# Graph attention layer on one core: q and k of the first stage made for all heads at once and placed by DMA, LayerNorm 1 applied on GpSimd

## The chip, the core and the metric

The kernel runs on one core of one Trainium2 chip. The metric is device time in microseconds of one whole execution. The engines are TensorE (PE; its weight loads are shown as PEld), VectorE (DVE), ScalarE (ACT), GpSimd (POOL) and SyncE (SP). Each runs its own list of instructions in order, and they wait for one another by semaphores. DMAs are issued here by SP and by ACT.

## The reference, cut to what matters

The input is x (4096 x 128, float32) and a 4096 x 4096 integer adjacency matrix. There are 8 heads of 16.

```
qkv = layer_norm(x, g1, be1) @ w_qkv            # q, k, v: 4096 x 8 x 16
scores = einsum('nhd,mhd->hnm', q, k) * HEAD_DIM ** -0.5
attn = softmax(where(adj != 0, scores, -inf))   # over m
x = x + einsum('hnm,mhd->nhd', attn, v).reshape(n, DIM) @ w_proj + b_proj
out = x + gelu(layer_norm(x, g2, be2) @ w1 + b1) @ w2 + b2
```

## The kernel before

**Two parts.** A first stage makes what all later work needs: k of all 4096 rows (`k_stack`), v (`v_ones`), q of the first tile (`q_stack[0]`), the normalized rows transposed (`xnT_dram`) and the masks and row maxima of the first tile. After it, `run_iterations` goes over 8 tiles of 512 query rows. This part is not touched.

**How q and k lie.** Products are taken in float16 with each number split in a high and a low part. A pair of heads lies in 128 partitions, 64 for each head: rows 0 to 15, 16 to 31 and 35 to 50 of a half hold copies of the head's 16 numbers, high or low as `Q_LOW` and `K_LOW` say (`PART_ROW` gives the first rows), and rows 32 to 34 serve a shift by the row maximum. In `k_stack` two of those rows hold the constant `SHIFT_UNIT`. Each chunk of 512 keys in `k_stack` has 64 more columns ahead (`K_FIRST`), a second copy of some keys.

**The first stage before.** The rows are taken in 8 chunks of 512. Per chunk: DVE takes mean and variance (`stats1`), ACT the root (`root`, L695), DVE applies them (`apply1`, four instructions of 128x128, L368), PE transposes (`transpose_rows`, L1055), ACT copies with scale and bias (`transposed_rows`, L701) and stores the chunk to `xnT_dram`. Then PE multiplies it by a weight matrix in which a pair's columns are repeated in the layout above (`wk_rep`, L1105), once for each of the 4 pairs: an "item". ACT reads each item twice (L722 the negated high part, L724 the float32 number), and POOL adds the two into `k_stack` (L543, and L541 for the 64 more columns). The first q takes 4 items more, so there are 36. PE also makes v (`chunk_values`), which ACT copies (L727).

**What else runs there.** POOL turns 12 blocks of 128x1024 adjacency numbers into masks (`convert`, two instructions, L517 and L521), one after every second item; DVE makes the first four (`first_masks`, L873). SP loads the blocks into two buffers (L407) and transposes masks by DMA (L412). For the row maxima of the first tile PE makes scores of 128 rows by 512 keys (`first_row`, L1080), and DVE takes the masked maximum of each (`row_maximum`, L858): 8 such units per chunk, 7 steps behind the items (`ROW_LAG`). At the end come `negated_maxima` (L868), 20 units of row maxima more, and the first tile.

**The order** of each engine is that of the loops as written: there is no scheduler. An instruction that waits holds all behind it on its engine, and a DMA is issued in its place in the list of the engine that issues it.

## Time and profile before

| | |
|---|---|
| median of 3 runs | 1702.24 us (1699.94 to 1702.98) |
| the profiled execution | 1704.14 us, of which the span is 1702.3 us |
| busy in the span: PE, DVE, ACT, POOL | 93%, 83%, 75%, 69% |
| DMA moved | 125.88 MB |

The span goes from the first instruction to the last. The page divides it into 40 slices, so that the first stage, which ends near 105 us, is two and a half of them. Shares over the whole span say little on it; the rows below are therefore of windows. The page puts an idle time down to the engine that released it.

### The profile page before, as it was taken

To read this page: it belongs to the slowest core of one execution; us is meant where nothing else is said; L and a number is where in the kernel's file an instruction comes from. 1 tells how busy PE (TensorE), PEld (TensorE's weight loads), DVE (VectorE), ACT (ScalarE), POOL (GpSimd) and SP (SyncE) were. 2 spreads that over 40 slices of the span, in tenths; PEclk is the share of its full clock that TensorE was granted. 3 is DMA by queue.
4 is the path that set the end of the run, shared out by engine and by line. 5 is a ranking of instruction groups with operands and counts; after the bars stand their busy time and mean duration, and the time that the engine had idled before them with its cause. 6 is when DMAs were issued, how large, how long until landed. Compare 5 with 4: busy or idle time off the path is not lost.

```text
span 1702.3 us, 46524 instructions
## 1 busy us (share of the span) xinstructions
PE 1588.7 (93%) x17016; PEld 496.5 (29%) x17016; DVE 1419.3 (83%) x4490; ACT 1274.2 (75%) x1394; POOL 1167.4 (69%) x1092
## 2 busy tenths in 40 slices
PE   6989999999999999999999999999999999999996
PEld 3422222323223232232323232232323232232323
DVE  6888989987999889997898879998899879988811
ACT  4647878777777878778776877778787787868793
POOL 4955487569865798568875698567885688657551
PEclk9979999999999999999999999999999999999997
DMA  8810046301460046500462025700464015600000
GB/s 214 184 52 2 5 142 128 76 5 57 141 124 30 5 116 138 97 5 26 137 127 63 5 81 136 134 2 5 133 130 88 4 39 148 123 18 5 14 5 13
DMA packets 177856, 125.88 MB, mean 74 GB/s; under 512 B 140974, under 2 KB 155183, under 8 KB 177628
## 3 DMA queue, kind: packets, MB, share of 16 engines
q1 hardware_dynamic: 163196, 108.49, 26.7%
q10 hardware_dynamic: 14432, 14.42, 3.3%
q8 instruction: 135, 2.21, 0.5%
q14 instruction: 93, 0.76, 0.1%
HBM read 77.25 MB, written 6.04 MB: 49 GB/s over the span
## 4 chain that ended last, share of the span: by engine, by line
PE 52%; ACT 22%; issue 14%; POOL 8%; DVE 2%; ACTq 1%; DMA 1%; SPq 0%; POOLq 0%; DVEq 0%
ACT probs L820 20%; PE pv_ps L1149 15%; PE ring_ps L1080 10%; PE score_ps L1241 9%; PE score_ps L1256 9%; POOL probs L582 2%; PE ring_ps L1207 2%; PE score_ps L1173 2%; POOL k_stack L543 2%; ACT q_stack L689 1%; DVE masked_out L858 1%; PE ring_ps L1198 1%; PE ring_ps L1183 1%; PE ring_ps L1190 1%; POOL row_mask L517 1%
## 5 line engine op out<-in xcount | busy, mean ns | idle before, releaser
L858 DVE CUSTOM_DVE_ANT_0 masked_out<-ring_ps,row_mask 128x512 bf16<-128x512 f32 x2048 | 1311.9, 688 | 138.6 <-PE ring_ps L1080 99.3
L820 ACT ACTIVATE probs<-score_ps,score_scale 128x1024 f32<-128x1024 f32 x1010 | 1075.6, 1112 | 338.5 <-PE score_ps L1256 324.4
L582 POOL TENSOR_TENSOR probs<-probs,keep 128x1024 int32<-128x1024 int32 x256 | 604.2, 2361 | 252.1 <-ACT probs L820 241.6
L1149 PE MATMUL pv_ps<-probs,v_ones 128*17 128x512 f32 x4096 | 543.7, 599 | 4.6 <-POOL probs L582 4.0
L1080 PE MATMUL ring_ps<-k_stack,q_stack 51*64 51x512 f16 x4096 | 488.0, 397 | 15.1 <-DVE row_max L858 13.8
L1256 PE MATMUL score_ps<-q_stack,k_stack 51*64 51x512 f16 x4040 | 370.4, 391 | 18.9
L1080 PEld LDWEIGHTS ring_ps<-k_stack,q_stack 51*64 51x64 f16 x4096 | 169.0, 104 | 495.7 <-DVE row_max L858 446.2
L1241 PE MATMUL score_ps<-mask_t,ident_bf 64*64 64x512 bf16 x3028 | 274.9, 387 | 34.1 <-ACT probs L820 15.5
L1256 PEld LDWEIGHTS score_ps<-q_stack,k_stack 51*64 51x64 f16 x4040 | 115.6, 104 | 211.6 <-PE score_ps L1241 183.6
L858 DVE DVE_READ_ACCUMULATOR2_ANT row_max<- 128x1 f32 x2048 | 169.9, 83 | 0.0
L521 POOL TENSOR_SCALAR row_mask<-row_mask 128x1024 bf16<-128x1024 bf16 x124 | 129.5, 1045 | 23.6 <-POOL row_mask L517 23.0
L1241 PEld LDWEIGHTS score_ps<-mask_t,ident_bf 64*64 64x64 bf16 x3028 | 91.9, 105 | 182.8 <-ACT probs L820 134.1
L517 POOL TENSOR_SCALAR row_mask<-adj_in 128x1024 bf16<-128x1024 uint32 x124 | 129.0, 1040 | 4.2 <-DVE row_max L858 2.1
L1149 PEld LDWEIGHTS pv_ps<-probs,v_ones 128*17 128x17 f32 x4096 | 72.4, 95 | 141.7 <-issue 73.6
L526 POOL TENSOR_SCALAR max_unit<-neg_max 128x4 f32<-128x4 f32 x64 | 12.7, 198 | 78.8 <-DVE neg_max L868 78.1
L958 DVE RECIPROCAL recip<-ring_ps 128x16 f32<-128x16 f32 x16 | 4.1, 257 | 61.0 <-PE ring_ps L1183 61.0
L689 ACT COPY q_stack<-score_ps 2x256 f16<-2x256 f16 x128 | 46.5, 363 | 9.2 <-PE score_ps L1047 6.9
L975 DVE TENSOR_TENSOR rows<-ring_ps,x_res 128x128 f32<-128x128 f32 x32 | 9.3, 291 | 41.1 <-PE ring_ps L1207 41.1
L574 POOL TENSOR_SCALAR keep<-mask_t 128x512 int32<-128x512 bf16 x64 | 39.6, 619 | 5.4
L1173 PE MATMUL score_ps<-h2T,w_sb 128*128 128x512 f32 x64 | 38.0, 688 | 2.4 <-ACT h2T L755 1.0
L591 POOL TENSOR_SCALAR q_x<-q_x 128x512 f32<-128x512 f32 x14 | 8.7, 620 | 45.2 <-ACT q_x L765 45.1
L722 ACT ACTIVATE hidden<-score_ps,part_coef 128x512 f16<-128x512 f32 x36 | 28.0, 777 | 14.5 <-PE score_ps L1105 11.8
(128 smaller groups left out, 840.3 us busy)
## 6 DMA issues: line engine op xcount, KB each, us to landing
adj_in<-adj SPq DMA_DIRECT2D x128, 512.0 KB, 4.2
halves<-attn ACTq DMA_DIRECT2D x30, 128.0 KB, 2.7
q_stack<-q_dram SPq DMA_DIRECT2D x42, 64.0 KB
mask_t<-row_mask SPq DMA_TRANSPOSE x128, 3.5
xq<-xnT_dram ACTq DMA_DIRECT2D x8, 256.0 KB, 2.7
halves<-halves ACTq DMA_DIRECT2D x16, 128.0 KB, 2.2
x_res<-x ACTq DMA_DIRECT2D x8, 256.0 KB, 4.5
out<-rows ACTq DMA_DIRECT2D x8, 256.0 KB, 5.4
```

The source lines that it names most:

```text
L517: nc.gpsimd.tensor_scalar(target, adj_in[:, half, :].bitcast(U32), 1.0, 0.0, ALU.min, ALU.max)\
L521: nc.gpsimd.tensor_scalar(target, target, BIG, -BIG, ALU.mult, ALU.add).then_inc(mask_done, 1)
L574: nc.gpsimd.tensor_scalar(keep[:, KEPT.index(m), :], mask_t[:, m, :], 1.0 / BIG, 1.0, ALU.mult, ALU.add)\
L582: nc.gpsimd.tensor_tensor(view, view, keep[:, KEPT.index(m), :].unsqueeze(1).broadcast_to([128, 2, TILE]), ALU.mult).then_inc(probs_masked, 1)
L689: last = nc.scalar.copy(stack[r:r + SHIFT_PARTS, p, 256 * jj:256 * (jj + 1)], bank.bitcast(F16)[r:r + SHIFT_PARTS, 0:256])
L820: nc.scalar.activation(probs[:, (2 * g + n) % SLOTS, :], score_banks(i, place).rearrange("p a n -> p (a n)"), ACT.Exp, scale=score_scale[: ...
L858: nc.vector.tensor_tensor_reduce(out=masked_out[:, place % 3, :], in0=ring_ps[:, place % 3, :], in1=row_mask[:, j, ch * 512:(ch + 1) * 512 ...
L1080: last = nc.tensor.matmul(ring_ps[64 * t:64 * (t + 1), place % 3, :], stack[rows, p, first:first + 64], k_stack[rows, p, ch, K_FIRST:], st ...
L1149: last = nc.tensor.matmul(pv_ps[32 * k:32 * k + HD + 1, :], v_ones[:, block_of(g, b), 2 * p + a, :], probs[:, (2 * g + b) % SLOTS, a * TIL ...
L1173: last = nc.tensor.matmul(bank, w1_sb[:, 128 * f:128 * (f + 1)], h2T[:, :], start=True, stop=True)
L1241: last = nc.tensor.matmul(bank[to, :], ident_bf[keys, keys], mask_t[keys, source, :], start=True, stop=False)
L1256: last = nc.tensor.matmul(bank[64 * t:64 * (t + 1), :], k_stack[rows, p, m // 4, at + 64 * t:at + 64 * (t + 1)], q_stack[par][rows, p, :], ...
```

## The change

Items are now 9: one for q of the first chunk and one for k of each chunk, each a product with the plain weight matrix (`wq_all`, `wk_all`), all heads at once, 128 rows of 16 x 8 numbers. ACT copies the product twice (high part in float16, and the float32 number), POOL subtracts to get the low part, ACT stores both parts to `item_dram`, and loads them from there into the rows of `q_stack[0]` (6 DMAs) or `k_stack` (9 DMAs for a chunk, 3 of them for the 64 more columns). The constant rows of `k_stack` are set once by DVE and copied over by two DMAs; `q_stack[0]` is cleared by DVE. The four instructions that apply LayerNorm 1 move from DVE to POOL. The masks that POOL makes come in pairs after an item. The row maxima run 8 steps behind instead of 7, and there are 4 steps to a chunk as before. The six instructions that filled the repeated weights, and POOL's clearing of them, are gone. The diff, cut:

```
+FIRST_PER = 4
+ITEMS = 1 + CHUNKS
 DEPTH = 4
-ROW_LAG = 7
+ROW_LAG = 8
-POOL_FIRST_MASKS = {4 + 2 * k: 4 + k for k in range(CONVERTED - 4)}
+POOL_FIRST_MASKS = {n: (2 * n + 2, 2 * n + 3) for n in range(1, 7)}
...
+            def apply1(c):
+
+                pool.wait_ge(rstd_done, c + 1)
+                if c >= 2:
+                    pool.wait_ge(stage_full, 2 * (c - 2) + 1)
+                settled(pool)
+                for s in range(SUB):
+                    nc.gpsimd.tensor_scalar(xn_rows[c % 2][:, s, :], x_all[:, c * SUB + s, :], mean_var[:, s, 0:1],
+                                            rstd[:, s:s + 1], ALU.subtract, ALU.mult).then_inc(ln1_applied, 1)
+
+            apply1(0)
             for n in range(ITEMS):
...
                 pool.wait_ge(item_read, n + 1)
...
-                nc.gpsimd.tensor_tensor(dst, item_x[n % DEPTH], item_neg[n % DEPTH], ALU.add).then_inc(item_done, 1)
...
+                nc.gpsimd.tensor_tensor(item_part[n % DEPTH][1], item_x[n % DEPTH], item_part[n % DEPTH][0],
+                                        ALU.subtract).then_inc(item_done, 1)
+                if n < CHUNKS - 1:
+                    apply1(n + 1)
+                for k in POOL_FIRST_MASKS.get(n, ()):
...
+            def take_item(n):
+
+                act.wait_ge(item_full, n + 1)
+                if n >= DEPTH:
+                    act.wait_ge(item_stored[n - DEPTH], 32)
+                nc.scalar.copy(item_part[n % DEPTH][0], score_ps[:, n % 4, :])
+                nc.scalar.copy(item_x[n % DEPTH], score_ps[:, n % 4, :]).then_inc(item_read, 1)
+
+            def store_item(n):
+                act.wait_ge(item_done, n + 1)
+                for low in range(2):
+                    act.dma_start(item_dram[n, low], item_part[n % DEPTH][low]).then_inc(item_stored[n], 16)
+
+            def load_item(n):
+
+                act.wait_ge(item_stored[n], 32)
+                for m, first in enumerate(PART_ROW):
+                    low = Q_LOW[m] if n == 0 else K_LOW[m]
+                    heads = item_dram[n, low].rearrange("(p a d) n -> a d p n", a=2, d=HD)
+                    for a in range(2):
+                        rows = slice(HALF * a + first, HALF * a + first + HD)
+                        to = q_stack[0][rows, :, :] if n == 0 else k_stack[rows, :, n - 1, K_FIRST:]
+                        act.dma_start(to, heads[a]).then_inc(item_in[n], 16)
+                    if n > 0:
+                        act.dma_start(k_stack[rows, :, n - 1, 0:K_FIRST],
+                                      heads[1][:, :, 128 * 2 + 64:128 * 3]).then_inc(item_in[n], 16)
...
+            for c in range(CHUNKS):
+                transposed_rows(c)
+                if c == 1:
+                    load_item(0)
+                if c >= 1:
+                    load_item(c)
+                if c + 1 < CHUNKS:
                     root(c + 1)
...
+                if c == 0:
+                    take_item(0)
+                take_item(c + 1)
+                act.wait_ge(stage_full, 2 * c + 2)
+                nc.scalar.copy(v_ones[:, c * SUB:(c + 1) * SUB, :, 0:HD],
+                               pv_ps[:, :].rearrange("p (s h d) -> p s h d", s=SUB, h=HEADS)).then_inc(v_done, 1)
+                if c == 0:
+                    store_item(0)
+                store_item(c + 1)
+            load_item(CHUNKS)
...
             for a in range(2):
-                nc.vector.memset(q_stack[1][HALF * a + SHIFT_ROW:HALF * (a + 1), :, :], 0.0).then_inc(q_clear, 1)
+                nc.vector.memset(k_stack[HALF * a + SHIFT_ROW:HALF * (a + 1), 0, 0, :], SHIFT_UNIT).then_inc(unit_set, 1)
+                for stack in q_stack:
+                    nc.vector.memset(stack[HALF * a + SHIFT_ROW:HALF * (a + 1), :, :], 0.0).then_inc(q_clear, 1)
...
                 if st >= ROW_LAG:
                     ch, j = divmod(st - ROW_LAG, SUB)
-                    pe.wait_ge(item_done, PAIRS * (ch + 1) + 1)
+                    if st == ROW_LAG:
+                        pe.wait_ge(unit_in, 32)
+                        pe.wait_ge(item_in[0], 16 * (Q_LOADS - 2))
+                    if j == 0:
+                        pe.wait_ge(item_in[ch + 1], 16 * (3 * len(PART_ROW)))
```

ACT's list before, from one transposed chunk to the next (chunk 2 to chunk 3; `hidden` and `probs` are the item's two copies, `attn` and `halves` the transposed chunks):

```order
L701 ACTIVATE halves<-pv_ps,gb 128x512 [waits stage_full]
L704 DMA xnT_dram<-halves 128x512 [waits xnT_ready]
L722 ACTIVATE hidden<-score_ps,part_coef 128x512 [waits item_done,item_full]
L724 COPY probs<-score_ps 128x512
L695 ACTIVATE rstd<-inv_var 128x4 [waits ln1_step]
L722 ACTIVATE hidden<-score_ps,part_coef 128x512 [waits item_done,item_full]
```

The same place in the list of the changed kernel, up to the stores of the next item:

```order
L705 ACTIVATE halves<-pv_ps,gb 128x512 [waits stage_full]
L708 DMA xnT_dram<-halves 128x512 [waits xnT_ready]
L732 DMA k_stack<-item_dram 16x4x512 [waits item_stored2]
L732 DMA k_stack<-item_dram 16x4x512
L734 DMA k_stack<-item_dram 16x4x64
L732 DMA k_stack<-item_dram 16x4x512 x2
L734 DMA k_stack<-item_dram 16x4x64
L732 DMA k_stack<-item_dram 16x4x512 x2
L734 DMA k_stack<-item_dram 16x4x64
L699 ACTIVATE rstd<-inv_var 128x4 [waits ln1_step]
L715 CAST hidden<-score_ps 128x512 [waits item_full]
L716 COPY probs<-score_ps 128x512
```

The root of the next chunk (L699) now stands behind a wait for the item's stores and nine DMA issues. After it come L761 (v) and the two stores L721, of which the first waits for POOL's `item_done`.

POOL's list before, over one mask (`hidden`, `probs` as above):

```order
L541 TENSOR_TENSOR k_stack<-probs,hidden 128x64 [waits item_read]
L543 TENSOR_TENSOR k_stack<-probs,hidden 128x512
L517 TENSOR_SCALAR row_mask<-adj_in 128x1024 [waits adj_loaded1]
L521 TENSOR_SCALAR row_mask<-row_mask 128x1024 [waits flag_done]
L541 TENSOR_TENSOR k_stack<-probs,hidden 128x64 [waits item_read]
L543 TENSOR_TENSOR k_stack<-probs,hidden 128x512
```

And POOL's list in the changed kernel, from the subtraction of item 2 to that of item 3 (`x_res` holds the normalized rows of chunk 3):

```order
L545 TENSOR_TENSOR hidden<-probs,hidden 128x512 [waits item_read]
L538 TENSOR_SCALAR x_res<-probs,mean_var,rstd 128x128 [waits rstd_done,stage_full]
L538 TENSOR_SCALAR x_res<-probs,mean_var,rstd 128x128 x3
L513 TENSOR_SCALAR row_mask<-adj_in 128x1024 [waits adj_loaded0]
L517 TENSOR_SCALAR row_mask<-row_mask 128x1024 [waits flag_done]
L513 TENSOR_SCALAR row_mask<-adj_in 128x1024 [waits adj_loaded1]
L517 TENSOR_SCALAR row_mask<-row_mask 128x1024 [waits flag_done]
L545 TENSOR_TENSOR hidden<-probs,hidden 128x512 [waits item_read]
```

Between two subtractions stand the four applications, which wait for ACT's root, and a pair of masks.

## Rows read from the trace of the kernel before

**Rows 1.** Busy time by window, us: PE, PEld, DVE, ACT, POOL, clock, DMA share, GB/s.
```profile
30.00:86.00 56.00, 51.20 (x270) 23.93 (x270) 49.67 (x154) 35.28 (x62) 52.24 (x65) 0.91 0.79 183
```

**Rows 2.** Groups of POOL up to 110 us: shapes, count | busy us, mean ns | idle before.
```profile
L543 POOL TENSOR_TENSOR k_stack<-probs,hidden 128x512 f16<-128x512 f32 x32 | 37.1, 1158 | 0.0
L521 POOL TENSOR_SCALAR row_mask<-row_mask 128x1024 bf16<-128x1024 bf16 x12 | 12.6, 1047 | 2.3 <-POOL row_mask L517 2.3
L517 POOL TENSOR_SCALAR row_mask<-adj_in 128x1024 bf16<-128x1024 uint32 x12 | 12.5, 1043 | 0.0
L541 POOL TENSOR_TENSOR k_stack<-probs,hidden 128x64 f16<-128x64 f32 x32 | 9.8, 306 | 6.6 <-ACT probs L724 5.6
```

**Rows 3.** Timeline of the first stage, start us, us: one mask on POOL, next item.
```profile
30.85 1.04 POOL L517 TENSOR_SCALAR row_mask<-adj_in 128x1024 bf16<-128x1024 uint32 x1
32.08 1.05 POOL L521 TENSOR_SCALAR row_mask<-row_mask 128x1024 bf16<-128x1024 bf16 x1 [0.19 <-POOL row_mask L517]
33.21 0.31 POOL L541 TENSOR_TENSOR k_stack<-probs,hidden 128x64 f16<-128x64 f32 x1
```

**Rows 4.** Timeline of the start and the end of the first stage.
```profile
19.24 0.20 ACT L695 ACTIVATE rstd<-inv_var 128x4 f32<-128x4 f32 x1 [1.89 <-DVE inv_var L364]
16.79 0.69 DVE L873 TENSOR_SCALAR row_mask<-adj_in 128x1024 bf16<-128x1024 int32 x1 [4.34 <-DMA adj_in<-adj]
101.72 1.15 POOL L543 TENSOR_TENSOR k_stack<-probs,hidden 128x512 f16<-128x512 f32 x1
103.78 0.69 DVE L858 CUSTOM_DVE_ANT_0 masked_out<-ring_ps,row_mask 128x512 bf16<-128x512 f32 x1
104.39 0.08 DVE L858 DVE_READ_ACCUMULATOR2_ANT row_max<- 128x1 f32 x1
```

**Rows 5.** DVE's application of LayerNorm 1: alone, and beside POOL (timeline).
```profile
10.47 1.11 DVE L368 TENSOR_SCALAR rows<-probs,mean_var,rstd 128x128 f32<-128x128 f32 x4
71.51 3.52 DVE L368 TENSOR_SCALAR rows<-probs,mean_var,rstd 128x128 f32<-128x128 f32 x4
```

**Rows 6.** One line's instructions: count, ns min/median/max; POOL's application of LayerNorm 2.
```profile
L631 POOL TENSOR_SCALAR rows<-x_res,mean_var,rstd x28: 787/791/798, 357.8 to 1539.4; 128x128 f32<-128x128 f32 x28
```

**Rows 7.** DMA issues, the same view, each with its issues' time to landing.
```profile
L704 ACTq DMA_DIRECT2D xnT_dram<-attn x4: 326/329/359, 14.0 to 67.5; - x4
DMA to landing us min/median/max: 2.0/3.1/5.5
...
L787 ACTq DMA_DIRECT2D halves<-attn x15: 614/620/1547, 225.5 to 1599.2; - x15
DMA to landing us min/median/max: 2.5/2.9/6.2
```

**Rows 8.** Timeline of SP: six loads of q from DRAM in the layout of the stacks.
```profile
233.02 3.50 SPq L484 DMA_DIRECT2D q_stack<-q_dram  x6
1410.79 2.69 SPq L484 DMA_DIRECT2D q_stack<-q_dram  x6
```

**Rows 9.** Groups of ACT and DVE up to 110 us.
```profile
L724 ACT COPY probs<-score_ps 128x512 f32<-128x512 f32 x36 | 20.8, 578 | 0.0
L701 ACT ACTIVATE attn<-pv_ps,gb 128x512 f32<-128x512 f32 x4 | 3.1, 784 | 10.8 <-PE pv_ps L1055 10.8
L914 DVE MEMSET q_stack<- 32x1024 uint32 x2 | 1.8, 912 | 1.3 <-PEq L1308 1.0 <-issue 0.3
```

**Rows 10.** Timeline of the first work of POOL and DVE.
```profile
3.36 0.87 DVE L356 BATCH_NORM_STATS2 stats<-probs 128x6 f32<-128x128 f32 x4 [0.27 <-DMA probs<-x]
17.43 1.15 POOL L543 TENSOR_TENSOR q_stack<-probs,hidden 128x512 f16<-128x512 f32 x1 [14.83 <-ACT probs L724]
```

More of the change, by code:

```diff
@@ L312, in program @@
         wqkv = probs[:, 5, 0:3 * DIM]
-        wq_rep = probs[:, 5, 3 * DIM:3 * DIM + PAIRS * 128].rearrange("p (q r) -> p q r", r=128)
         xn_rows = [rows2[:, :, :], x_res[:, :, :]]
         xnT = [attn[:, 0, :], attn[:, 1, :], halves[:, 0, :], halves[:, 1, :]]
-        item_neg = [hidden[:, n // 2, 256 * (n % 2):256 * (n % 2) + 256].bitcast(F16) for n in range(DEPTH)]
+        item_part = [[hidden[:, 2 * low + n // 2, 256 * (n % 2):256 * (n % 2) + 256].bitcast(F16) for low in range(2)]
+                     for n in range(DEPTH)]
         item_x = [probs[:, 6 + n // 2, TILE * (n % 2):TILE * (n % 2) + TILE] for n in range(DEPTH)]
@@ L364, in layer_norm_stats @@
             nc.vector.reciprocal(inv_var[:, :], inv_var[:, :]).then_inc(chain, 1)
-        def layer_norm_apply(chain, src, dst):
-            for s in range(SUB):
-                nc.vector.tensor_scalar(dst[:, s, :], src[:, s, :], mean_var[:, s, 0:1], rstd[:, s:s + 1],
-                                        ALU.subtract, ALU.mult).then_inc(chain, 1)
         def settled(eng):
@@ L706, in _ @@
+            act.wait_ge(unit_set, 2)
+            for a in range(2):
+                own = k_stack[HALF * a + SHIFT_ROW:HALF * a + SHIFT_ROW + SHIFT_PARTS + 1, :, :, :]\
+                    .rearrange("r p c k -> r (p c) k")
+                act.dma_start(own[:, 1:, :], own[:, 0:1, :].broadcast_to([SHIFT_PARTS + 1, PAIRS * CHUNKS - 1, K_CHUNK]))\
+                  .then_inc(unit_in, 16)
             root(0)
-            act.wait_ge(q_clear, 2)
+            act.wait_ge(q_clear, 4)
             act.wait_ge(w_in, 16 * 5)
-            act.wait_ge(consts_in, 16 * 4)
+            act.wait_ge(consts_in, 16 * 3)
@@ L924, in _ @@
             for st in range(FIRST_STEPS):
-                blk, k = st // PAIRS, st % PAIRS
+                blk, k = divmod(st, FIRST_PER)
                 if k == 0 and blk + 1 < CHUNKS:
@@ L929, in _ @@
                     first_masks(DVE_MASKS[st])
-                if k == 2 and blk + 1 < CHUNKS:
-                    apply1(blk + 1)
                 if st >= ROW_LAG:
@@ L1087, in first_row @@
                 row_scores(q_stack[0], u, j, p, a, ch)
-            pe.wait_ge(q_clear, 2)
+            pe.wait_ge(q_clear, 4)
             pe.wait_ge(scale_step, 4)
@@ L1092, in _ @@
             nc.tensor.matmul(score_ps[:, 0, 0:2 * DIM], ones_mat, w_sq, start=True, stop=True).then_inc(bound_full, 1)
-            pe.wait_ge(consts_in, 16 * 4)
-            pe.wait_ge(w_rep, 2 * len(PART_ROW) + 3)
+            pe.wait_ge(consts_in, 16 * 3)
+            pe.wait_ge(w_rep, 4)
             transpose_rows(0)
             for st in range(FIRST_STEPS):
-                blk, p = st // PAIRS, st % PAIRS
+                blk, p = divmod(st, FIRST_PER)
                 if p == 0 and 1 <= blk < CHUNKS:
                     transpose_rows(blk)
-                if st < ITEMS:
-                    chunk = max(blk - 1, 0)
-                    pe.wait_ge(xnT_ready, chunk + 1)
-                    if st >= 4:
-                        pe.wait_ge(item_read, st - 3)
-                    nc.tensor.matmul(score_ps[:, st % 4, :], (wq_rep if blk == 0 else wk_rep)[:, p, :],
-                                     xnT[chunk % 4], start=True, stop=True).then_inc(item_full, 1)
+                if p == 1 and blk < CHUNKS:
+                    pe.wait_ge(xnT_ready, blk + 1)
+                    for n in ((0, 1) if blk == 0 else (blk + 1,)):
+                        if n >= 4:
+                            pe.wait_ge(item_read, n - 3)
+                        nc.tensor.matmul(score_ps[:, n % 4, :], wq_all[:, :] if n == 0 else wk_all, xnT[blk % 4],
+                                         start=True, stop=True).then_inc(item_full, 1)
                 if st >= ROW_LAG:
                     ch, j = divmod(st - ROW_LAG, SUB)
-                    pe.wait_ge(item_done, PAIRS * (ch + 1) + 1)
+                    if st == ROW_LAG:
[3 more added lines that the diff above has]
+                        pe.wait_ge(item_in[ch + 1], 16 * (3 * len(PART_ROW)))
                     for x in range(2):
@@ L1114, in _ @@
                     chunk_values(blk).then_inc(stage_full, 1)
-            pe.wait_ge(item_done, ITEMS)
+            pe.wait_ge(item_read, ITEMS)
             for g in range(-LEAD, 0):
@@ L1289, in constants @@
 def constants():
-    c = np.zeros((128, 136), np.float32)
+    c = np.zeros((128, 132), np.float32)
     c[:, 0:128] = np.eye(128)
@@ L1293, in constants @@
         c[32 * k + HD, 128 + k] = 1.0
-    for r in range(128):
-        for n, first in enumerate(PART_ROW):
-            if first <= r % HALF < first + HD:
-                c[r, 132] = -Q_LOW[n]
-                c[r, 133] = -K_LOW[n]
-        if SHIFT_ROW <= r % HALF < SHIFT_ROW + SHIFT_PARTS:
-            c[r, 135] = SHIFT_UNIT
     return c
```

66 lines of the change are left out of this document (15 added, 51 removed).

## The prediction, made before the changed kernel was run

> **What bounds the kernel now.** The change touches only the first stage, so I read that stage and leave the tiles alone. First the windows: from 30 to 86 us, where the stage runs evenly, POOL is busy 52.24 of 56 us and DVE 49.67, ACT only 35.28 [rows 1]. Then the groups: POOL has 32 k items of 1.158 + 0.306 us and 12 masks [rows 2]. A mask takes 2.36 us from its start to the next instruction, 33.21 - 30.85 [rows 3]. A chunk costs POOL 4 x 1.46 + 1.5 x 2.36 = 9.4 us and the stage runs POOL nearly without a gap: its last item begins at 101.72, and the last of the row maxima that the stage gates ends at 104.39 + 0.08 = 104.47 us [rows 4]. So POOL bounds the stage now, with DVE close behind, and the change takes work from both. The question is what the time from 19.24 us, when the root of chunk 1 is taken [rows 4], to 104.47 us becomes.
>
> **What is removed.** POOL's items fall from 36 to 9, DVE loses 4 instructions a chunk that take 1.11 us alone and up to 3.52 us beside POOL [rows 5], ACT loses most of its item copies. By busy time alone the stage would be much shorter.
>
> **What is added, and where it stands.** ACT now issues for every chunk 2 stores and 9 loads, and it must wait for the stores to land before it loads. POOL has the four applications. Both are in order, and the order closes a circle through both engines. For chunk c: ACT takes the root of c; POOL, which waits for it, applies; POOL makes its pair of masks; only then POOL subtracts item c; ACT, which holds at the end of its step for this subtraction, stores the two parts; ACT copies the transposed chunk, waits for the landing, issues nine loads; and only behind these stands the root of c+1. Nothing in this circle lies beside another part of it, save ACT's copy beside the DMA's flight.
>
> **The circle in numbers.**
> - Application: 4 x 0.791 = 3.2 us, from POOL's same instruction on the same shape in LayerNorm 2, which varies only from 787 to 798 ns [rows 6].
> - Masks: 2 x 2.36 = 4.7 us [rows 3]. Their adjacency blocks were asked for a circle earlier, so no wait.
> - Subtraction: 1.16 us, that of L543 [rows 2], say 1.2.
> - Stores and landing: 0.1 for the semaphore, 0.5 for the first issue, and 3.0 from the second issue to landing: 3.6 us. ACT's own work meanwhile is two issues, the copy of 0.784 [rows 9] and its store of 0.33, about 2.3 us, and is covered. The landing is bounded from both sides by ACT's own queue: 2.0 to 5.5 us for 256 KB stores, 2.5 to 6.2 for 128 KB moves, medians 3.1 and 2.9 [rows 7]. I take 3.0. With 2.0 ACT's own 2.3 us would decide, 1.3 less; with 5.5, 2.5 more.
> - Nine loads: not in the trace on ACT. The nearest in form are SP's six loads of q, 2.69 to 3.50 us for six, so 0.45 to 0.58 each [rows 8]; ACT's own issues lie at 0.33 for whole tiles and 0.62 for the second of two half tiles [rows 7]. I take 0.48, nearest to the q loads: 4.3 us. Bounds 9 x 0.37 = 3.3 (0.33 and a gap) and 9 x 0.64 = 5.8.
> - Root and hand-over: 0.3 us.
> Sum 3.2 + 4.7 + 1.2 + 3.6 + 4.3 + 0.3 = 17.3 us a chunk. Before, the whole stage gave (104.47 - 19.24) / 8 = 10.7.
>
> On the landing, the Trainium skill (DMA: Bandwidth & Descriptors, "Anatomy of one DMA") puts one DMA at about 2.0 us fixed plus its bytes at 436 GB/s, on GpSimd's path. For 128 KB this gives 2.3 us, by which the circle would be 0.7 shorter and the sum below some 5 us less; the trace's medians of 2.9 and 3.1 [rows 7] are above it, with other queues busy.
>
> **The beginning.** The root of chunk 1 still comes at 19.24, as DVE waits for the second adjacency block till 16.79 before it [rows 4]. What is new ahead of it is hidden: two more clearings of 0.912 [rows 9] and two smaller ones push the first statistics from 3.36 [rows 10] to about 6, the application is in POOL's empty time (it is idle 14.83 us ahead of 17.43 [rows 10]), and chunk 0 has some 4 us to spare. If that cover is gone, for example because POOL needs longer for its first work, it costs up to 9 us. Then: two items copied, the first by 20.5 (2 x 0.578 [rows 9]); subtraction to 21.7; application to 24.9; second subtraction to 26.1; stores and transposed copy to 28.3; 6 + 9 loads of 0.48, 7.2 us, to 35.5; root 35.8; application 39.0; masks 43.7; item 2 is subtracted at 44.9.
>
> **The run and the end.** Items 3 to 7 follow at 17.3: 44.9 + 5 x 17.3 = 131.4. Then, with no masks and no application left: stores and landing 3.6, loads of chunk 6's keys 4.3, two copies 1.1, subtraction 1.2, stores and landing 3.6, nine loads 4.3, landing of the last 2.5 past its issue: 20.6, at 152.0. Then PE 0.4 and eight row maxima at the pitch of 0.61 (104.39 - 103.78 [rows 4]), 4.9: 157.3 us, where before stands 104.47. All behind it (negated maxima, 20 units, tiles) has the same instructions in the same order, and nothing there had waited for the first stage's other products: the last loads and mask transposes land while the row maxima run. So the change costs 52.8 us. Of the profiled execution's own 1704.14 us (span 1702.3 and 1.8 around it) that makes 1757; on the median of 1702.24, 1.9 lower, 1755. I give 1755.
>
> DVE's wait grows to half of each circle: it has 8 x 0.61 = 4.9 us of maxima and under 2 of statistics a chunk. PE is idle more, so its granted clock may be at its lower level here, as it partly is already (0.91 mean [rows 1]). Neither lies in the circle: PE's transposes run beside POOL's masks, its v beside ACT's loads.
>
> On moving the application, POOL's 3.2 us stands against 1.11 alone and 3.52 beside POOL on DVE [rows 5]: the step itself becomes no shorter, and it is now in the circle. The Trainium skill (Perfetto Trace Analysis, "Optimizing Scalar/DVE Operations") warns that GpSimd and VectorE share an SBUF port, so that moving work between the two might not help. The trace agrees, the same four instructions being three times as long beside POOL; it changes no term, since POOL's durations are what the sum uses.
>
> **Rivals.**
> - *The hand-over is cheap.* Issues of 0.37, landing inside ACT's own 2.3 us: the circle is 1.0 + 1.3 = 2.3 shorter, 7 landings and 7 ninefold loads behind item 2 make 16, the 15 loads ahead 1.7. The cost falls to 35: 1737. For it: the 0.33 of the whole-tile issues. Against: all strided issues on the two queues are 0.45 or more.
> - *The queue is crowded.* Issues of 0.64 and landings of 5.5: 1.5 + 2.5 more in seven places and 2.4 ahead, 30 more: 1785. For it: one L787 took 1.547 to issue and one landing 6.2 [rows 7], and the DMA engines are busy 0.79 of the time [rows 1]. Against: adjacency blocks and mask transposes are the bulk of that, and come once per circle, which makes them sparser; they are issued during POOL's masks, when ACT only waits.
> - *The other side: the circle is open.* If the loads do not hold ACT (issue overlaps, landing already past), POOL's own 3.2 + 4.7 + 1.2 = 9.1 us sets the pace from the second subtraction at 26.1: six chunks to 80.7, then a short end of two copies, subtraction, two landings of 2.0 and the row maxima, 11.5: 92.2, 12.3 us less than 104.47, so 1690. For it: busy times, which all fall. Against: the root's place behind the nine loads in ACT's list, and that issues are seen to take ACT's time in order. The point from which it decides is where the circle falls to about 17.3 - 52.8 / 7 = 9.8 us: that leaves 0.7 us for all that ACT does in it, and I count 8.2.
> - *The extra is made good later*, because the tiles start with work that was late anyway. Against: the last row maximum of the stage is followed directly by the negated maxima.
>
> **How the numbers follow.** The circle as summed, 1743 to 1770: 0.69. Cheap hand-over, near 1737: 0.10. Crowded, near 1785: 0.13. Open circle, 1690: 0.06. Made good later, near 1702: 0.02. The range that holds 8 in 10 takes the main case and most of its two neighbours, 1735 to 1783. A run of this kernel can be told from no change by about 0.2%, 3.4 us: faster 0.06, within it 0.02, slower 0.92.
>
> **What would show it.** ACT's nine issues in a row of about 0.48 each, then the root, then POOL's four applications of 0.79, the pair of masks and the subtraction with ACT idle meanwhile; a period of 17.3 us between subtractions; POOL idle some 8 us in each, DVE idle more than half; last row maximum ahead of the negated maxima at 157 us, and the rest of the span unchanged. Wrong would be: a root that is taken before the loads are issued, subtractions 10 us or less apart, a landing wait of over 5 us or issues of over 0.7 as a rule, or a first application that ends after 16 us.

## The result, and the profile after

| | before | after |
|---|---|---|
| median | 1702.05 us (4 runs) | 1771.93 us (4 runs, 1771.09 to 1773.03) |
| profiled execution, and its span | 1704.14, 1702.3 us | 1771.95, 1770.1 us |
| ratio of the times | | 1.0413 [1.0395, 1.0431] |

The change costs 69.9 us. The forecast was 52.8 (1755 us, range 1735 to 1783). In the first stage every engine is less busy than before. The window of the even part of the first stage, which answers to [rows 1] (same columns: PE, PEld, DVE, ACT, POOL, clock, DMA share, GB/s), in the profile after:

```profile
30.00:86.00 56.00, 27.62 (x118) 14.51 (x118) 17.60 (x70) 7.37 (x15) 23.01 (x26) 0.50 0.58 145
```

POOL falls from 52.24 to 23.01 us, DVE from 49.67 to 17.60, ACT from 35.28 to 7.37, and in the same 56 us far less of the stage gets done. PE's granted clock is 0.50, its lower level. No engine bounds this stage any more: they wait for one another in a ring. One turn of it, ACT's timeline in the profile after (start us, us; a "q" marks DMA issues, and the idle time counts compute alone, so the issues lie in it):

```profile
90.48 0.87 ACTq L721 DMA_DIRECT2D item_dram<-hidden  x2
91.45 0.78 ACT L705 ACTIVATE attn<-pv_ps,gb 128x512 f32<-128x512 f32 x1 [8.71 <-POOL hidden L545]
92.26 0.33 ACTq L708 DMA_DIRECT2D xnT_dram<-attn  x1
94.82 0.80 ACTq L732 DMA_DIRECT2D k_stack<-item_dram  x2
95.66 0.45 ACTq L734 DMA_DIRECT2D k_stack<-item_dram  x1
...
98.52 0.45 ACTq L734 DMA_DIRECT2D k_stack<-item_dram  x1
99.01 0.21 ACT L699 ACTIVATE rstd<-inv_var 128x4 f32<-128x4 f32 x1 [6.78 <-issue]
```

And POOL's timeline ahead of it:

```profile
81.47 3.14 POOL L538 TENSOR_SCALAR rows<-probs,mean_var,rstd 128x128 f32<-128x128 f32 x4 [9.18 <-ACT rstd L699]
84.58 1.04 POOL L513 TENSOR_SCALAR row_mask<-adj_in 128x1024 bf16<-128x1024 uint32 x1
...
89.30 1.15 POOL L545 TENSOR_TENSOR hidden<-probs,hidden 128x512 f16<-128x512 f32 x1
```

The reader should see four things in a row: POOL waits 9.18 us for the root, applies, makes its masks, subtracts; ACT then stores, and from 92.59 to 94.82 does nothing at all until the stores have landed; then come nine issues of about 0.46 us; and only behind them the next root. The subtractions of items 2 to 7 start at 51.67, 71.13, 89.30, 107.30, 126.24 and 146.06 us, 18.9 us apart on the mean.

The stage's last row maximum ends at 173.86 + 0.08 = 173.94 us, where 104.47 stood [rows 4]:

```profile
173.25 0.69 DVE L892 CUSTOM_DVE_ANT_0 masked_out<-ring_ps,row_mask 128x512 bf16<-128x512 f32 x1
173.86 0.08 DVE L892 DVE_READ_ACCUMULATOR2_ANT row_max<- 128x1 f32 x1
```

That is 69.5 us later, and the span is 67.8 longer. All the loss is in the first stage, and the tiles behind it take the same time within 1.7 us.

### The profile page after: what moved, and what is told of

It is laid out like the page before. It is cut to its first block, busy times and chain, and to the rows that moved or that the text cites. A ratio compares the mean times of both kernels' runs of the same rounds, so it can differ in the third digit from the quotient of the medians.

```text
span 1770.1 us, 46333 instructions
## 1 busy us (share of the span) xinstructions
PE 1586.9 (90%) x16962; PEld 496.1 (28%) x16962; DVE 1404.3 (79%) x4457; ACT 1240.7 (70%) x1340; POOL 1154.8 (65%) x1063
## 4 chain that ended last, share of the span: by engine, by line
PE 49%; ACT 21%; issue 14%; POOL 8%; DMA 3%; ACTq 2%; DVE 2%; SPq 0%; POOLq 0%; DVEq 0%
ACT probs L858 19%; PE pv_ps L1180 14%; PE ring_ps L1107 10%; PE score_ps L1272 9%; PE score_ps L1287 9%; POOL probs L586 2%; PE ring_ps L1238 2%; DMA item_dram<-hidden 2%; PE score_ps L1204 2%; ACT q_stack L693 1%; DVE masked_out L892 1%; ACTq L732 1%; PE ring_ps L1229 1%; PE ring_ps L1214 1%; DMA adj_in<-adj 1%
## 5 line engine op out<-in xcount | busy, mean ns | idle before, releaser
L1107 PE MATMUL ring_ps<-k_stack,q_stack 51*64 51x512 f16 x4096 | 496.2, 404 | 17.9 <-DVE row_max L892 11.0
L1272 PE MATMUL score_ps<-mask_t,ident_bf 64*64 64x512 bf16 x3028 | 275.1, 387 | 34.8 <-ACT probs L858 17.4
L699 ACT ACTIVATE rstd<-inv_var 128x4 f32<-128x4 f32 x8 | 1.7, 207 | 58.2 <-issue 48.3
```

The costliest lines, as they stand in the source:

```text
L1107: last = nc.tensor.matmul(ring_ps[64 * t:64 * (t + 1), place % 3, :], stack[rows, p, first:first + 64], k_stack[rows, p, ch, K_FIRST:], st ...
L1272: last = nc.tensor.matmul(bank[to, :], ident_bf[keys, keys], mask_t[keys, source, :], start=True, stop=False)
```

## The experiments

The theory after the result: the ring sets the pace, and a later start, longer landings and slower issues than forecast make up the 17 us that the forecast lacked. The rivals: the placement by DMA is itself slow, whatever the order; or the move of LayerNorm 1 to GpSimd is what costs. Four kernels each take one piece out of the changed kernel.

**The root ahead of the loads** (`root_early`).

```
                 transposed_rows(c)
+                if c + 1 < CHUNKS:
+                    root(c + 1)
                 if c == 1:
                     load_item(0)
                 if c >= 1:
                     load_item(c)
-                if c + 1 < CHUNKS:
-                    root(c + 1)
```

> The changed kernel with one edit: ACT takes the root of the next chunk before it waits for the item's stores and issues the nine loads, not behind them. Theory (one circle of waits through ACT and POOL, 18.9 us a chunk in the changed kernel's trace): application and masks on POOL (7.9 us) then run beside landing, loads and copies on ACT (9.7 us), the circle falls to about 12 us, item 2 is subtracted 7 us sooner and five circles are 6.9 us shorter: some 41 us less, 1731 us. Rival (the DMA queues are the bound: landings stretch when the same traffic must go in less time; the DMA engines' share of 0.6 at 18.9 us a circle is 11.5 us of work): landings of 6 us and more, circle of 14 or above, 1743 or more.

Measured: 1734.42 us (1732.11 to 1738.19), ratio to before 1.0197 [1.0178, 1.0216]. That is 37.5 less than after. The subtractions of items 2 to 7 now start 12.5 us apart. The same nine loads, with the same landings of the stores (median 4.4 us), cost 6.4 us a chunk less when the root stands ahead of them. So the order of ACT's list, and not the DMAs' own time alone, makes over half of the loss. The gain stops there, for another ring stands behind it. This is the chain of waits of this kernel between 60 and 85 us (start us, us, what):

```profile
63.52 0.21 ACT rstd L699
...
71.77 1.17 POOL hidden L545
72.96 0.34 ACTq L721
73.34 4.28 DMA item_dram<-hidden
77.63 0.33 ACTq L732
...
82.38 0.58 ACT hidden L715
82.96 0.50 ACT probs L716
83.50 0.13 issue
83.64 1.17 POOL hidden L545
```

In this stretch the landing and the nine issues are still between two subtractions, as ACT's copies of the next item stand behind the loads.

**The masks ahead of the application** (`masks_first`).

```
+                for k in POOL_FIRST_MASKS.get(n, ()):
+                    if k == 4:
+                        pool.wait_ge(mask_done, 4)
+                    convert(k % SUB, k // SUB, k % 2, k // 2 + 1, k - 4)
                 if n < CHUNKS - 1:
                     apply1(n + 1)
-                for k in POOL_FIRST_MASKS.get(n, ()):
-                    if k == 4:
-                        pool.wait_ge(mask_done, 4)
-                    convert(k % SUB, k // SUB, k % 2, k // 2 + 1, k - 4)
```

> The changed kernel with one edit: POOL makes its pair of masks straight behind a subtraction, ahead of the next application, where it idles 9 to 12 us for the root. Theory (circle): the masks' 4.7 us leave the circle six times, 28 us less, 1744 us. Rival (crowded queue): the masks release adjacency loads and mask transposes just when ACT's stores fly, landings grow by 2 to 2.5 us, and only half is won: 1757 us.

Measured: 1739.27 us (1737.38 to 1741.13), 1.0223 [1.0206, 1.0241], 32.7 less than after. POOL now makes the masks in the time in which it waited for the root. The masks were 4.7 us of the circle, and it shrank by 5.2, to 13.7 (items 2 to 7). So the masks' own time is nearly all of the gain. Two things that I had not thought of nearly cancel behind it. One is the stores' time from issue to landing, which fell. This is the view of the store's line, in the profile after and then in this kernel:

```profile
L721 ACTq DMA_DIRECT2D item_dram<-hidden x18: 327/412/502, 27.1 to 160.7; - x18
...
DMA to landing us min/median/max: 1.7/4.0/7.0
```

```profile
L721 ACTq DMA_DIRECT2D item_dram<-hidden x18: 326/396/631, 26.9 to 127.3; - x18
...
DMA to landing us min/median/max: 1.7/2.0/6.6
```

After the change, SP's load of the next adjacency block (512 KB) and a transpose are issued 2 us ahead of the stores: SP's timeline after, to be laid beside ACT's 90.48 above.

```profile
88.01 0.33 SPq L406 DMA_DIRECT2D adj_in<-adj  x1
88.45 1.33 SPq L411 DMA_TRANSPOSE mask_t<-row_mask  x1
```

In this kernel the stores go out first (61.91, the block's load 62.92). That fits the shorter landing, but no run changes this order alone. The other is the nine loads, which take back most of it: from the first to the root 5.5 us on the mean of the five circles and not 4.7 (at most 6.4, from 64.18 to 70.59).

**The constant rows' DMAs later** (`units_late`). They were ACT's first work; they now follow the stores of item 1.

```
-            act.wait_ge(unit_set, 2)
-            for a in range(2):
-                own = k_stack[HALF * a + SHIFT_ROW:HALF * a + SHIFT_ROW + SHIFT_PARTS + 1, :, :, :]\
-                    .rearrange("r p c k -> r (p c) k")
-                act.dma_start(own[:, 1:, :], own[:, 0:1, :].broadcast_to([SHIFT_PARTS + 1, PAIRS * CHUNKS - 1, K_CHUNK]))\
-                  .then_inc(unit_in, 16)
...
                 store_item(c + 1)
+                if c == 0:
+                    act.wait_ge(unit_set, 2)
...
```

> The changed kernel with one edit: the two DMAs that copy the constant rows of k_stack are issued behind the first items' stores instead of ahead of everything. Theory: these two, from and to three partitions each, held the adjacency loads of the start (the second landed at 22.2 us instead of 16.8), so the root of chunk 1 comes back from 24.6 to about 19.3 us: 5.4 us less, 1766.5 us. Rival: DVE's longer clearing or the later statistics did it; then the root stays at 24.6 us and the time at 1772 us.

Measured: 1773.36 us (1772.39 to 1775.46), 1.0425 [1.041, 1.0441]: nothing gained. Yet the cause was right. After the change DVE's second mask waited for its block till 22.16, where it had been 16.79 [rows 4]; the two copies of the constant rows (three partitions each, broadcast over 31 places) were in the queues from 4.35 on. The two profiles' rows of that, after and then here:

```profile
4.35 2.16 ACTq L742 DMA_DIRECT2D k_stack<-k_stack  x2
...
24.61 0.21 ACT L699 ACTIVATE rstd<-inv_var 128x4 f32<-128x4 f32 x1 [9.34 <-DVE inv_var L368]
```

```profile
19.65 0.20 ACT L699 ACTIVATE rstd<-inv_var 128x4 f32<-128x4 f32 x1 [4.49 <-DVE inv_var L368]
...
30.97 2.58 ACTq L708 DMA_DIRECT2D xnT_dram<-attn  x1
33.59 5.93 ACTq L732 DMA_DIRECT2D q_stack<-item_dram  x6
...
43.87 0.21 ACT L699 ACTIVATE rstd<-inv_var 128x4 f32<-128x4 f32 x1 [12.93 <-issue]
```

The root of chunk 1 is back at 19.65. But where the two copies are now, all behind them is slow: a single issue holds ACT for 2.58 us, the next six for 5.93, and the root of chunk 2 comes at 43.87, after the change at 43.40. The burden was moved, not removed.

**The application back on VectorE** (`apply_on_dve`), with the items still placed by DMA.

```
-                    nc.gpsimd.tensor_scalar(xn_rows[c % 2][:, s, :], x_all[:, c * SUB + s, :], mean_var[:, s, 0:1],
-                                            rstd[:, s:s + 1], ALU.subtract, ALU.mult).then_inc(ln1_applied, 1)
...
+                    nc.vector.tensor_scalar(xn_rows[c % 2][:, s, :], x_all[:, c * SUB + s, :], mean_var[:, s, 0:1],
+                                            rstd[:, s:s + 1], ALU.subtract, ALU.mult).then_inc(ln1_applied, 1)
...
+                if k == 2 and blk + 1 < CHUNKS:
+                    apply1(blk + 1)
```

> The changed kernel with LayerNorm 1 applied on DVE again, at the place that it had before (items placed by DMA, alone). Theory (circle): subtraction and masks of POOL no longer wait for the root; what is left in the circle is ACT's own list (stores 1.0, landing to 4.3, nine loads 4.2, root 0.2, copies 1.1) and the subtraction 1.2, so 12 to 12.5 us: 1730 to 1735 us. Rival: loads and landings alone are the price and POOL's work lay beside them anyway: circle still above 17, about 1770 us.

Measured: 1732.92 us (1730.62 to 1734.14), 1.0182 [1.0163, 1.02]. The move to GpSimd costs 39.0 us on top of the items by DMA, which by themselves cost 30.9. So both halves of the change hurt. With the application on DVE POOL makes its masks while it would have waited, which takes out of the ring what `masks_first` takes out: the circle is 12.7 us here and 13.7 there.

**The other half alone** (`apply_pool_alone`): the kernel before, its 36 items as they were, but LayerNorm 1 applied on POOL.

```
+                    nc.gpsimd.tensor_scalar(xn_rows[c % 2][:, s, :], x_all[:, c * SUB + s, :], mean_var[:, s, 0:1],
+                                            rstd[:, s:s + 1], ALU.subtract, ALU.mult).then_inc(ln1_applied, 1)
...
             for n in range(ITEMS):
                 blk, p = n // PAIRS, n % PAIRS
+                if p == 2 and blk + 1 < CHUNKS:
+                    apply1(blk + 1)
```

> The kernel before with one part of the change alone: the four applications of LayerNorm 1 of each chunk on POOL, items made as before. Theory (POOL bounds that stage): its 3.16 us for each of chunks 1 to 7 come on top of 9.4 us a chunk, 22 us, less about 2 us of gaps that it had: 20 us more, 1722 us. Rival (DVE, relieved of 2.1 to 3.5 us a chunk, gives most of it back): less than 8 us more, 1710 us or below.

Measured: 1721.95 us (1720.12 to 1723.73), 1.0126 [1.0109, 1.0143], so 21.5 more than before (1700.47). POOL was the full engine: 7 x 3.2 = 22 us more work on it in the stage, 21.5 us more time. Its window, to be read against POOL's 52.24 of 56 in [rows 1]:

```profile
40.00:100.00 60.00, 44.48 (x220) 19.26 (x219) 35.34 (x121) 30.56 (x52) 57.20 (x72) 0.87 0.63 141
```

Here the Trainium skill's warning (Perfetto Trace Analysis, "Optimizing Scalar/DVE Operations": moving work between GpSimd and VectorE may not help, as they share a port) is borne out, though by plainer means than a port: POOL had 4 us in 56 to spare.

**More issues** (`extra_issues`): the changed kernel with six more loads a chunk, of 8 KB each, ahead of the root. They go into a DRAM tensor that nothing reads.

```
+                if n > 0:
+                    for m in range(6):
+                        act.dma_start(extra_dram[n, m], heads[1][:, :, 128 * 2 + 64:128 * 3]).then_inc(extra_in, 16)
```

> The changed kernel with six more small loads for each chunk (8 KB each, into a DRAM tensor that nothing reads), issued by ACT behind the nine. Theory (an issue holds ACT, and the root is behind it): 6 x 0.475 = 2.85 us in each of the seven circles, 20 us more, 1792 us. Rival (issues lie beside a landing or POOL's work): no more than 5 us, 1777 us or below.

Measured: 1800.18 us (1797.93 to 1801.0), 1.0584 [1.0568, 1.06], which is 28.3 more than after. Seven chunks times what the six issues hold ACT make 27:

```profile
88.72 3.79 ACTq L739 DMA_DIRECT2D extra_dram<-item_dram  x6
92.56 0.20 ACT L700 ACTIVATE rstd<-inv_var 128x4 f32<-128x4 f32 x1 [10.94 <-issue]
```

An issue costs what it holds its engine, here 0.63 us, though it moves only 8 KB. I had expected 0.48 for each.

**The constant rows by VectorE** (`units_by_dve`): two DVE memsets of 3x9216 float32 words in place of the two copies.

```
-                act.dma_start(own[:, 1:, :], own[:, 0:1, :].broadcast_to([SHIFT_PARTS + 1, PAIRS * CHUNKS - 1, K_CHUNK]))\
-                  .then_inc(unit_in, 16)
...
+                if st in (3, 5):
+                    r = HALF * (st // 2 - 1) + SHIFT_ROW
+                    nc.vector.memset(k_stack[r:r + SHIFT_PARTS + 1, :, :, :].rearrange("r p c k -> r (p c k)").bitcast(F32),
+                                     float(np.uint32(0x78007800).view(np.float32))).then_inc(unit_set, 1)
```

> The changed kernel, with the constant rows of k_stack written by two long clearings on DVE in its idle time (steps 3 and 5) instead of two DMAs. In the run that only issued the two DMAs later the root of chunk 1 did come 5 us sooner (19.65 us), but the issues behind them on ACT took up to 2.6 us each, and the root of chunk 2 stood at 43.87 us as before. Theory (the two DMAs keep the queues for some 10 us wherever they stand): without them the root of chunk 2 comes at 36 to 38 us, 1764 to 1767 us. Rival (the start is bound elsewhere): 1771 us.

Measured: 1766.61 us (1764.66 to 1768.51), 1.0389 [1.0373, 1.0404]: 5.3 less than after, at the price of two DVE instructions of 7.7 us in DVE's idle time. The kernel before was 1.6 us faster in this series (1700.47 us) than in that of the result, so against its own comparison the gain is 3.7. The traces say the same: the root of chunk 1 comes at 20.14, 4.5 us earlier than after the change, and the stage's last row maximum ends 4.3 us earlier, at 169.61. So the start's term by itself is 4 to 5 us, most of the 5.4 by which that root was late. The run also leaves out DVE's two short clearings of `k_stack` at the very start (0.54 us each).

**Can the order be mended?** `root_masks_units` takes three edits together: root early, masks first, constant rows by DVE.

> The changed kernel with three of the four mends: constant rows by DVE, masks ahead of the application, root ahead of the loads; the item's copies stay behind the loads. Theory (circles, each open at one place): sum of the single gains, 5 + 33 + 38, would be 1696 us; but the circle through landing, loads, copies and subtraction stays, 2.9 + 4.2 + 1.1 + 1.2 and some waiting, 10.5 to 12 us: 1715 to 1725 us. Rival (each mend takes the same slack): no better than the better of the two, 1734 less 5, 1729 us.

Measured: 1727.47 us (1726.72 to 1731.22), 1.0154 [1.0135, 1.0173]. `all_mended` adds a fourth, ACT's copies of the next item ahead of the loads of the last:

```
                 take_item(c + 1)
+                if c == 1:
+                    load_item(0)
+                if c >= 1:
+                    load_item(c)
                 act.wait_ge(stage_full, 2 * c + 2)
```

> The changed kernel with the constant rows by DVE, masks ahead of the application, the root ahead of the loads, and the item's copies ahead of the loads too, so that no wait closes the circle. Theory: now busy time sets the pace. If it is POOL's 9.1 us a chunk, item 7 is subtracted near 81 us and the last row maximum of the stage ends near 99 us: 1697 us. If it is the DMA engines (0.90 busy at 11.9 us a chunk in the run with the root early, 10.7 us of work), item 7 comes near 92 us and the stage ends near 110 us: 1708 us. Rival (the placement by DMA costs more than it saves in any order): above 1712 us.

Measured: 1729.34 us (1724.79 to 1730.27), 1.0164 [1.0147, 1.0182]. The two can't be told apart, and both are far above the 1697 to 1708 us that the expectation of `all_mended` worked out from busy times. The ring through the root and POOL is gone here, and the chain of waits of `all_mended` shows a new one:

```profile
42.22 5.78 DMA k_stack<-item_dram
...
48.13 0.64 PE ring_ps L1104 x4
48.78 2.02 PE score_ps L1129 x2
```

PE's row-maximum scores for a chunk wait for the last load of it to land, 5.78 us after its issue, and the product for the next item stands behind them on PE. `more_lag` was to open this ring: the row maxima run 12 steps behind the items and not 8, and POOL shares the constant rows.

```
-ROW_LAG = 8
+ROW_LAG = 12
...
+            units(nc.gpsimd, 1, 0, PAIRS // 2, pool_units)
...
             apply1(0)
...
+            units(nc.gpsimd, 0, 0, PAIRS, pool_units)
```

> The run all_mended with the row maxima 12 steps behind instead of 8 and the constant rows written by POOL (in its two first idle times) and DVE. In all_mended the trace shows a second circle: PE's first row of a chunk waits 6 to 7 us for the last load to land, the product of the next item stands behind it on PE, and ACT's copies and loads behind that, 13.4 us a chunk with PE at half its clock. Theory (that circle): with a chunk more of lag no load is waited for, the pace falls to what POOL and the DMA engines need, 10 to 11 us, some 5 x 2.5 us and 4 us at the start less: 1708 to 1714 us. Rival (the DMA engines are the bound, 0.86 to 0.89 busy already): 1722 us or more.

Measured: 1730.4 us (1727.42 to 1732.36), 1.0164 [1.0148, 1.018]: no gain. Between 45 and 100 us the chain is now almost only the stores' landings and ACT's issues (shares of the stretch, then pieces of one turn):

```profile
by line: DMA item_dram<-hidden 72.1%; ACTq L746 21.2%; ACTq L748 12.9%; ACT v_ones L769 3.9%; issue 2.4%; ACTq L735 0.3%
...
43.09 8.42 DMA item_dram<-hidden
51.54 0.33 ACTq L746
...
56.11 0.43 ACT v_ones L769
56.57 8.47 DMA item_dram<-hidden
```

This is once more a ring, and all of it lies in ACT's own list: the landing of one item's stores, its nine loads (51.54 to 56.07), the copy of v, and only then the stores of the next item. Four turns of it, from 43.09 to 97.04, took 13.5 us each. `all_mended` has the same order: its copies moved ahead of the loads, but its stores did not. No run puts the loads of an item behind the stores of the next, so the obvious next mend is untested.

What makes this ring long is the landing. A store of 128 KB that needs 2.0 us by the median in `masks_first` needs 6.0 here, and 8.5 at most. The queues of the same kernel from 40 to 100 us (packets, MB, share of 16 engines; q1 is SP's, q10 ACT's), and then those of the kernel before from 30 to 86 us:

```profile
q1 hardware_dynamic: 14988, 7.98, 70.2%
q10 hardware_dynamic: 5724, 4.51, 35.1%
```

```profile
q1 hardware_dynamic: 15076, 8.63, 70.7%
q10 hardware_dynamic: 864, 1.57, 7.9%
```

Together 105% of the engines' time, at 209 GB/s (above 100% the packets' times must overlap). Before, an even stretch of the stage took 79%. That the engines are full, and that this makes the landings long, is only argued. Against it stand two things: `all_mended` took the same time at a share of 0.89, and `masks_first`, with the shortest landings, had nearly the share of this kernel. Its window from 40 to 100 us, and then that of the kernel after (the last three columns: clock, DMA share, GB/s), whose landings had a median of 4.0:

```profile
40.00:100.00 60.00, 39.15 (x168) 18.81 (x168) 28.02 (x103) 11.70 (x24) 35.98 (x40) 0.50 1.01 196
```

```profile
40.00:100.00 60.00, 28.45 (x122) 13.90 (x122) 20.86 (x74) 8.36 (x18) 25.86 (x28) 0.50 0.54 133
```

So the mean share alone does not tell how long a store takes to land. ACT's queue has 5724 packets for 4.5 MB, so about 790 bytes each. The Trainium skill (DMA: Bandwidth & Descriptors, "Issuing engines are not separate DMA queues") says that all DMAs end up on the same 16 engines, whoever issues them. The traces agree: with ACT's loads beside them SP's adjacency blocks land after 6.9 us here (median) and after 4.2 before.

**Does POOL alone set the pace of the kernel before?** It was the first statement of the forecast. In the kernel before, POOL's 32 additions of 64 columns (0.306 us each [rows 2]) were left to others: ACT copies the columns (`again_on_act`), or a DMA within `k_stack` does (`again_by_dma`).

```
-                if blk > 0:
-                    again = slice(128 * 2 + 64, 128 * 3)
-                    nc.gpsimd.tensor_tensor(k_stack[:, p, blk - 1, 0:K_FIRST], item_x[n % DEPTH][:, again],
-                                            item_neg[n % DEPTH][:, again], ALU.add)
...
+                nc.scalar.copy(k_stack[:, :, ch, 0:K_FIRST], k_stack[:, :, ch, first:first + K_FIRST]).then_inc(again_in, 1)
```

> The kernel before with one edit: the 64 more columns of each chunk of k_stack are copied from the finished chunk by ACT, one copy for all four pairs, in place of four additions on POOL (0.306 us each). Theory (POOL bounds the stage of the kernel before, with DVE next): POOL falls from 9.4 to 8.2 us a chunk, DVE's 9.2 then sets the pace, 1 us a chunk less: 8 us less than before, ratio 0.995. Rival (DVE and its waits for POOL's port already set the pace): less than 2 us.

Measured: 1702.64 us (12 runs), ratio 1.0002 [0.9992, 1.0011]. POOL has 1.2 us less to do in each chunk, which would make 9.8 us in all, and nothing comes of it:

```profile
30.00:86.00 56.00, 49.83 (x252) 22.46 (x250) 51.91 (x155) 35.32 (x64) 47.36 (x44) 0.91 0.85 185
```

POOL has fallen from 52.24 to 47.36, and DVE risen from 49.67 to 51.91. PE, at 51.20 before [rows 1], has 49.83. Where the chain of waits ran between 35 and 95 us, in the kernel before and then in this one:

```profile
by line: POOL k_stack L543 42.9%; POOL row_mask L517 18.7%; issue 16.7%; POOL k_stack L541 10.2%; POOL row_mask L521 8.5%; PE score_ps L1105 1.8%; PE ring_ps L1080 1.2%; POOLq L372 0.3%
```

```profile
by line: PE score_ps L1110 29.8%; PE ring_ps L1085 12.1%; DVE masked_out L863 9.9%; DVE x_res L369 8.9%; PE pv_ps L1074 8.6%; issue 7.1%; PE pv_ps L1076 6.0%; PE pv_ps L1060 4.2%; DVE rows L369 3.5%; PE pv_ps L1070 3.2%; DVE stats L357 2.6%
```

POOL had 80% of it and has none now; PE has 64% and DVE 25%. So a second path, through PE and DVE, was nearly as long as POOL's, and relief to POOL is worth nothing, while load on it costs in full. Which of the two bounds that path no run separates.

In `again_by_dma` the last line is instead:

```
+                act.dma_start(k_stack[:, :, ch, 0:K_FIRST], k_stack[:, :, ch, first:first + K_FIRST]).then_inc(again_in, 16)
```

> As the run again_on_act, but the 64 more columns are copied by one DMA a chunk from k_stack to k_stack, issued by ACT: the one piece of placement by DMA that nothing waits for until the tiles begin. Theory (POOL's time is what counts, and the DMA is off every path): as with ACT, 8 us less, ratio 0.995. Rival (512 pieces of 128 bytes crowd the DMA engines, which are 0.79 busy, and the adjacency blocks come late for POOL's masks): no gain, or up to 10 us more.

Measured: 1704.65 us (11 runs), 1.0017 [1.0008, 1.0025], slightly slower, with the stage's end 2.7 us later than before by the memset that follows it (107.28 and 104.58).

## Why the forecast was right, and what its size lacked

**The mechanism.** Right: the root stands behind nine issues, the landing lies in the ring, all engines idle in it, and the end of the stage moves while the tiles do not. `root_early` and `masks_first` show each of two links by taking it out, `extra_issues` shows the price of a third by adding to it.

**The circle, 17.3 us forecast, 18.9 measured.** Over the five circles between items 2 and 7, application, masks, subtraction and hand-over took 9.4 us, as summed. Two terms were too small:
- Stores and landing, 3.6 forecast: from the end of the subtraction to the first load 4.46, 4.33, 4.37, 4.29 and 6.19 us, mean 4.7. I took the landing's 3.0 from the medians of ACT's own DMAs before the change [rows 7]. These stores are issued each time behind the load of an adjacency block. The upper bound, 5.5, was passed twice at the end:

```profile
127.81 5.76 DMA item_dram<-hidden
...
147.66 5.99 DMA item_dram<-hidden
```

- Nine loads, 4.3 forecast: 4.2 us in two circles and 5.57 in the longest, where one pair of issues took 2.31 us; mean 4.7. The value per issue (0.48) was right for an issue that isn't held up.

**The budget of the 16.6 us** in the profile, between the forecast end of the stage, 157.3, and 173.94: the start 5.4 (root of chunk 1 at 24.61 and not 19.24), from there to item 2 28.2 and not 25.7, so 2.5 (one store of item 1 took 7.01 us to land), five circles 5 x 1.6 = 7.9, and the tail 0.8.

**The step that was wrong** is in "The beginning": "What is new ahead of it is hidden". I counted DVE's clearings and POOL's application there, and both were hidden indeed: the first application ended at 12.15, well before 16. I did not count the two copies of constant rows as transfers; the sum has them at nothing and gives no reason. They delayed the second adjacency block, and through it all that followed. `units_late` shows that they did, and `units_by_dve` that this was worth 4 to 5 us. The forecast held without this term because the range was wider than what it lacked.

**"POOL bounds the stage now, with DVE close behind"** was half right. POOL's list was the chain, but the words "close behind" mattered more than I gave them, and they left out PE: `again_on_act` shows that a path through PE and DVE is level with POOL's. For the forecast this changed nothing, as neither bounds the stage after.

**The rivals.** *Cheap hand-over*, 1737: no, issues are 0.46 and up. *Crowded queue*, 1785: partly true, as landings reach 5.8 to 7.0 us and single issues 1.8, but not in every circle; its landing was passed (5.76 us against 5.5) and its loads nearly reached (5.57 against 5.8), but never in the same circle: the longest took 19.8 us and not 21.3. *Open circle*, 1690: refuted for this order. Whether another order would open it is not shown: the best of those that were tried (`root_masks_units`) got down to 12.3 us a chunk and kept a ring through landing and loads. *Made good later*: refuted, 69.5 us at the stage's end stayed 67.8 in the span.

**PE's clock.** I had said that its lower level lies outside the circle. The changed kernel's four runs all have a mean clock of 0.944 or 0.945 over the span, the profiled one 0.50 in the stage, so they can't show its price. Other kernels were granted either level: the runs of `root_masks_units` with 0.995 to 0.997 took 1726.72 to 1727.61 us, the one with 0.955 took 1731.22, and `root_early` took 1732.11 and 1734.35 at 0.995 and more, 1734.49 and 1738.19 at 0.954. On the means that is 3 to 4 us in all, some 0.5 us a chunk: in those kernels it would be little of the 69.9.

**What stays open.** Why the landings grow when the transfers come closer together, and whether the DMA engines would bound the stage once no ring did. Counted by the share of the 16 engines, the kernel after needed 10.6 us of them for each 18.9 us circle (17.4% for ACT's queue and 38.9% for SP's, over the 100 us from 40 on), and `more_lag` 14.2 for each 13.5 (105.3%). So much the same transfers took more of the engines' time each. That packets from DRAM to few partitions get in one another's way is only argued; I made no run with other piece sizes, nor one with the loads behind the next stores. Nor was a version found that beats the kernel before: the best of those that place by DMA, `root_masks_units`, is 1.5% slower.

## What to carry to other kernels

Work taken off busy engines is worth nothing if what replaces it waits in order on another: write down, for each engine's list, what the new waits and issues stand ahead of, and follow that through the other engines until it closes. A DMA costs three things, the time that its issue holds the issuing engine, its landing, and its share of engines that every queue uses; price all three, the one-off transfers at the start included. Where two paths are nearly equally long, adding work to one costs all of it, and taking work off one brings nothing. And a mend opens one ring only: look in its trace for the next before the gain is counted.

## What the runs showed of the hardware

- The landing of one and the same 128 KB store had medians of 2.0 us (`masks_first`), 4.0 (after) and 6.0 (`more_lag`, at most 8.5). The mean share of the DMA engines did not order them: 1.01, 0.54 and 1.06 from 40 to 100 us. The Trainium skill (DMA: Bandwidth & Descriptors, "Anatomy of one DMA") gives 2.3 us by its formula, for the path through GpSimd. The runs lie on both sides of it: the shortest landing was 1.7 us, and the medians go from 2.0 to 6.0.
- Two copies from SBUF to SBUF that write only three partitions each, 2 issues of 1.1 us, delayed a 512 KB load issued 2 us later by some 5 us, or, put elsewhere, held the issuing engine for 2.58 us at the next single issue (`units_late`).
- An issue on ACT's queue took 0.33 us for a whole tile, 0.45 for a strided piece of 64 KB or 8 KB alike, 0.63 from DRAM to DRAM (`extra_issues`), and up to 2.6 behind the two copies (`units_late`), in which time ACT computed nothing.
